# A tower of attention and experts on one core: the two attention terms moved through two column halves of TensorE instead of one summed term

## What is computed

```python
q, k, v = (split_heads(x @ W + b) for W, b in ((Wq, bq), (Wk, bk), (Wv, bv)))
scores = einsum("bhqd,bhkd->bhqk", q, k) / sqrt(64)
scores = scores * where(int(abs(scores) * 1618) % 9 in (0, 3, 6), 1 / PHI, 1.0)
a = softmax(scores)
a = a * (sin(C1 * a) * exp(-(a * a) / PHI) + cos(C2 * a))      # C1 = 118.6, C2 = 1.94
h = h + concat_heads(a @ v) @ Wo + bo
```

## Time and profile before

| | us |
|---|---|
| median of 3 runs | 6793.55 |
| fastest, slowest of them | 6787.77, 19916.96 |
| the profiled execution | 6774.6 |
| its span | 6772.9 |

### The profile page before, as it was taken

The page is one execution under the profiler, slowest core; times in us unless marked ns, Lnnn a source line. Parts: engine busy times, 40 slices in busy tenths (PEclk is TensorE's granted clock), DMA queues, the critical chain, the costliest instruction groups (busy, mean ns, idle before and its releaser), DMA issues. The chain is left out here.

```text
span 6772.9 us, 115321 instructions
## 1 busy us (share of the span) xinstructions
PE 5442.1 (80%) x32426; PEld 3955.2 (58%) x32489; DVE 5082.3 (75%) x10177; ACT 4262.2 (63%) x7370; POOL 2754.5 (41%) x2639
## 2 busy tenths in 40 slices
PE   2788877787777877877888777778787799997999
PEld 1455555555555555555655555555555577775777
DVE  1888888888888888888888888888888555555443
ACT  1677777777777777777777777777777322222222
POOL 4445554444555544444555444445554200100111
PEclk9888898989889888888888889888988799898999
DMA  1000000000000000000000000000000000000000
GB/s 17 12 8 7 7 7 7 7 7 10 7 7 7 7 7 7 7 9 9 7 7 7 7 7 7 9 9 7 7 7 4 8 1 2 1 1 13 4 6 6
DMA packets 34500, 48.46 MB, mean 7 GB/s; under 512 B 24473, under 2 KB 24537, under 8 KB 34010
## 3 DMA queue, kind: packets, MB, share of 16 engines
q1 hardware_dynamic: 31962, 43.49, 2.5%
q0 software_dynamic: 2048, 0.14, 0.1%
HBM read 39.40 MB, written 4.19 MB: 6 GB/s over the span
## 5 line engine op out<-in xcount | busy, mean ns | idle before, releaser
L571 PE MATMUL banks<-ident,att 128*128 128x128 f32 x8192 | 1458.9, 311 | 873.6 <-DVE ag L508 496.8
L571 PEld LDWEIGHTS banks<-ident,att 128*128 128x128 f32 x8192 | 1024.2, 159 | 1568.6 <-DVE ag L508 1044.0
L377 POOL TENSOR_TENSOR sinb<-sinb,work 128x512 f32<-128x512 f32 x1024 | 1289.3, 1272 | 900.3 <-DVE sinb L482 898.3
L599 PE MATMUL banks<-kT,qT 128*128 128x512 f32 x2048 | 1262.5, 702 | 113.9 <-ACT att L423 104.0
L387 POOL TENSOR_SCALAR wgt<-wgt 128x512 f32<-128x512 f32 x1024 | 700.2, 684 | 1586.7 <-DVE wgt L502 1581.4
L635 PEld LDWEIGHTS outp<-vo,sinb 128*128 128x128 f32 x8192 | 1164.7, 216 | 214.9 <-issue 185.3
L635 PE MATMUL outp<-vo,sinb 128*128 128x64 f32 x8192 | 1162.6, 295 | 1.9 <-ACT att L423 1.9
L476 DVE TENSOR_TENSOR work<-banks,work 128x512 f32<-128x512 f32 x1024 | 699.8, 689 | 254.0 <-ACT work L435 183.6
L451 ACT ACTIVATE work<-banks 128x512 f32<-128x512 f32 x1024 | 609.9, 596 | 420.4 <-PE banks L571 411.6
L458 ACT ACTIVATE mag<-banks 128x512 f32<-128x512 f32 x1024 | 606.4, 594 | 356.2 <-PE banks L599 350.0
L435 ACT ACTIVATE work<-banks,halfpi 128x512 f32<-128x512 f32 x1024 | 695.4, 685 | 208.9 <-PE banks L571 139.6
(11 more groups left out here) (194 smaller groups left out, 6740.6 us busy)
## 6 DMA issues: line engine op xcount, KB each, us to landing
xq<-xT_dram SPq DMA_DIRECT2D x64, 256.0 KB
xv<-xT_dram SPq DMA_DIRECT2D x64, 256.0 KB, 3.7
xT_dram<-xT SPq DMA_DIRECT2D x8, 256.0 KB, 2.9
out<-hres SPq DMA_DIRECT2D x8, 256.0 KB, 2.6
base<-in_L_tok_turns,idx POOLq DMA_INDIRECT x64
wqk<-in_L_attn_Wq SPq DMA_DIRECT2D x64, 16.0 KB
wqk<-in_L_attn_Wk SPq DMA_DIRECT2D x64, 16.0 KB
wqk<-in_L_attn_bq SPq DMA_DIRECT2D x64, 0.2 KB
```

Source lines behind the costliest of these rows:

```text
L377: nc.gpsimd.tensor_tensor(sinb[:, k % RING], sinb[:, k % RING], work[:, k % RING], ALU.add).then_inc(summed, 1)
L571: mm = nc.tensor.matmul(bank[:, i * P:(i + 1) * P], att[:, p, 4 * half + i, kt * P:(kt + 1) * P], ident[:], is_transpose=True, start=(i == ...
L599: nc.tensor.matmul(score_bank(n), qT[:, p, (n // 2) * P:(n // 2 + 1) * P], kT[:, p, (n % 2) * 512:(n % 2 + 1) * 512], start=True, stop=Tru ...
```

## The change

The two terms are no longer summed on GpSimd. Both go into TensorE as moving operands of 512 columns, with `vo` of the key block (128 x 64) as the stationary one: `work` writes partitions 0 to 63 of `outp`, `sinb` partitions 64 to 127. Each of the two matmuls so uses one half of the array's columns. The result is transposed, 64 x 512 queries for each term, so one query half fills the bank, and tiles are taken half by half: tile k is key block k % 8 and query half k // 8, for Gauss and sine too. VectorE takes each half out of `outp` (semaphore `evac`) into `acc`; an even head copies, an odd one adds to it. After the odd head eight matmuls with `pair`, two identities one above the other, fold both terms and turn the result back into 128 queries x 64 (`folded`), and VectorE adds that into `hres`, once for two heads. 

kT exists once: an even head has its q and k in rows 0 to 63, an odd one in rows 64 to 127, and the other half of its qT is zeros, so scores contract over 128 rows, of which the other head's k meets zeros. A head's projection is therefore put behind the last score of the head before (24 and 26 instead of 18 and 20), with the wait for all 16 scores, and the values move from 25 to 29. The rings `work` and `sinb` are freed by `av`, not by the sum. The diff, cut to its core:

```diff
-        kT = sb("kT", [P, 2, S])
+        kT = sb("kT", [P, S])
+        acc = sb("acc", [P, 2, 512])
+        pair = sb("pair", [P, D])
...
-        PROJ, VAL = 18, 25 + STEPS
+        PROJ, VAL = 24, 29 + STEPS
...
-        AV = [SINE + 6 + 8 * k // 5 for k in range(NTILE)]
-        OUT = AV[-1] + 1
+        AV = [SINE + 6 + k if k < TB else SINE + 16 + 2 * (k - TB) for k in range(NTILE)]
+        OUT = (AV[TB - 1] + 1, AV[-1] + 1)
+        FOLD, ADD = OUT[1] + 1, OUT[1] + 2
...
-                        k = a - SINE - 5
-                        if 0 <= k < NTILE:
-
-                            wait(pool, tmul, NTILE * g + k + 1)
-                            nc.gpsimd.tensor_tensor(sinb[:, k % RING], sinb[:, k % RING], work[:, k % RING],
-                                                    ALU.add).then_inc(summed, 1)
...
-                    wait(act, qk, NTILE * (g - 1))
+                    wait(act, qk, NTILE * g)
                 cols = slice(c * 512, (c + 1) * 512)
-                nc.scalar.activation(qT[0:D, p, cols], outp[0:D], ACT.Copy, scale=QSCALE).then_inc(qk_sb, 1)
-                nc.scalar.activation(kT[0:D, p, cols], outp[D:P], ACT.Copy).then_inc(qk_sb, 1)
+                rows = slice(p * D, (p + 1) * D)
+                nc.scalar.activation(qT[rows, p, cols], outp[0:D], ACT.Copy, scale=QSCALE).then_inc(qk_sb, 1)
+                nc.scalar.activation(kT[rows, cols], outp[D:P], ACT.Copy).then_inc(qk_sb, 1)
...
-                        if a == OUT:
-                            wait(dve, av, NTILE * (g + 1))
+                        if a in OUT:
+                            half = OUT.index(a)
+                            wait(dve, av, NTILE * g + TB * (half + 1))
+                            if p == 0:
+                                nc.vector.tensor_copy(acc[:, half], outp[:]).then_inc(evac, 1)
+                            else:
+                                nc.vector.tensor_tensor(acc[:, half], outp[:], acc[:, half], ALU.add).then_inc(evac, 1)
+                        if a == ADD and p == 1:
+                            wait(dve, folded, folds(g, p) + 1)
                             hv = hres[:, bass.ds((g // H) * TB, TB), :]
                             nc.vector.tensor_tensor(hv, outp[:].rearrange("p (t d) -> p t d", d=D), hv,
                                                     ALU.add).then_inc(outd, 1)
...
                             wait(pe, acd, NTILE * g + k + 1)
-                            wait(pe, turned, TB * (g + 1))
-                            kt, half = k // 2, k % 2
+                            wait(pe, turned, TB * g + 4 * (k // TB) + 4)
+                            kt, half = k % TB, k // TB
...
-                            fill(g, p, gauss_bank(d), d // 2, d % 2)
+                            fill(g, p, gauss_bank(d), d % TB, d // TB)
...
-                            wait(pe, summed, NTILE * g + k + 1)
+                            kt, half = k % TB, k // TB
+
+                            wait(pe, acd, NTILE * g + k + 1)
+                            wait(pe, tmul, NTILE * g + k + 1)
                             if k == 0:
                                 wait(pe, v_sb, g + 1)
-                            kt, half = k // 2, k % 2
-                            for i in range(4):
-                                o = (4 * half + i) * D
-                                mm = nc.tensor.matmul(outp[:, o:o + D], sinb[:, k % RING, i * P:(i + 1) * P],
-                                                      vo[:, kt, :], start=(k == 0 and i == 0),
-                                                      stop=(k >= NTILE - 2), skip_group_check=True)
+                            if k == TB:
+                                wait(pe, evac, 2 * g + 1)
+                            for term, rows in ((work, slice(0, D)), (sinb, slice(D, P))):
+                                mm = nc.tensor.matmul(outp[rows], vo[:, kt, :], term[:, k % RING],
+                                                      start=(kt == 0), stop=(kt == TB - 1), skip_group_check=True)
                             mm.then_inc(av, 1)
+                        if a == FOLD and p == 1:
+                            wait(pe, evac, 2 * g + 2)
+                            for j in range(TB):
+                                mm = nc.tensor.matmul(outp[:, j * D:(j + 1) * D],
+                                                      acc[:, j // 4, j % 4 * P:(j % 4 + 1) * P], pair[:],
+                                                      start=True, stop=True)
+                            mm.then_inc(folded, 1)
```

More of the change, by code:

```diff
@@ L316, in stages, with folds @@
                     yield g, (par - stage) % 2, s + STEPS * stage
+        def folds(g, p):
+            if isinstance(g, int):
+                return g // 2
+            return (g - p) // 2
         def score_bank(n):
@@ L365, in _ @@
             pool.wait_ge(consts, 5)
-            nc.gpsimd.memset(qT[D:P], 0.0).then_inc(consts, 1)
+            nc.gpsimd.tensor_tensor(pair[:], ident[:, 0:D], ident[:, D:P], ALU.add).then_inc(consts, 1)
             pool.wait_ge(consts, 6)
-            nc.gpsimd.memset(kT[D:P], 0.0).then_inc(consts, 1)
+            nc.gpsimd.memset(qT[:], 0.0).then_inc(consts, 1)
+            pool.wait_ge(consts, 7)
+            nc.gpsimd.memset(kT[:], 0.0).then_inc(consts, 1)
             def iteration(t, par):
@@ L393, in _ @@
         def _(act):
-            act.wait_ge(consts, 7)
+            act.wait_ge(consts, 8)
             def projections(g, p, c):
@@ L433, in iteration @@
                             else:
-                                wait(act, summed, NTILE * g + k - RING + 1)
+                                wait(act, av, NTILE * g + k - RING + 1)
                             nc.scalar.activation(work[:, k % RING], sine_bank(k), ACT.Sin,
@@ L447, in iteration @@
                             if d < RING:
-                                wait(act, summed, NTILE * g - RING + d + 1)
+                                wait(act, av, NTILE * g - RING + d + 1)
                             else:
@@ L549, in _, with project @@
         def _(pe):
-            pe.wait_ge(consts, 7)
-            def project(g, c):
+            pe.wait_ge(consts, 8)
+            def project(g, p, c):
                 wait(pe, loadq, 80 * (g + 1))
                 if c == 0:
-                    wait(pe, outd, g - 2)
+                    wait(pe, evac, 2 * (g - 2))
+                    wait(pe, outd, folds(g - 2, p))
                 else:
@@ L643, in iteration @@
                             wait(pe, qk_sb, 4 * NHEADS if last else 4 * (g + 3))
-                            wait(pe, outd, g)
+                            wait(pe, evac, 2 * g)
+                            wait(pe, outd, folds(g, p))
                             for j in range(TB):
```

16 lines of the change are left out of this document (8 added, 8 removed).

## The result

The changed kernel takes 7148.85 us in the median of 4 runs (7129.88 to 7185.85) against 6790.66: ratio 1.0537, interval 1.0482 to 1.0593, slower by 358 us (the ratio leaves out the one run of the kernel before at 19916.96 us). 7275 had been forecast, in a range of 6920 to 7620.

What follows compares the result with a forecast made beforehand. No engine was full: VectorE bound the score and Gauss stretch, a ring across engines the sine stretch. Terms 5.9 + 0.9 - 0.6 + 0.5 + 0.9 = +7.6 us a head, times 63 +480 us: about 7275 us, range 6920 to 7620.

Steps and rivals of the forecast that it cites:

- the side of 2%: Whole kernel: 2%, 136 us, is about what a measurement can tell from no change; slower than that had chance 0.83.
- TensorE becomes the bound of eight sine steps: Sine stretch, first eight attention-value tiles: a TensorE step grows from 1.55 to 2.29 us, +5.9 us a head.
- The pair of matmuls: Attention-value tile: two column-half matmuls take 1.28 us, with 0.30 for the change of form 1.58 us a tile.
- A2 and B1: A and B are a tile's two matmuls, 1 and 2 their passes; only second of A and first of B overlap.
- rival 2: Attention-value matmuls: the column halves run wholly together, +3.6 us a head, about 7020 us; chance 0.18.
- Projections and values: Turn from Gauss to sine: projection copies move behind the last score and values move later, +0.9 us a head.
- the table load (1.28 us) and the first cosines cover that: Start of sine: value matmuls at s = 29 hold transposes and L586 behind them, but this is hidden; no cost added.
- Late tiles and fold: Score and Gauss stretch: tiles at s = 12 and 14 and the fold at s = 16, together +0.9 us a head.
- Order by halves: Gauss stretch: TensorE no longer waits at the second tile, but VectorE is the full engine there; 0, upper bound 0.
- Contention: VectorE's L497 beside GpSimd's L382: without the sums the scalings start earlier and stop slowing it, -0.6 us a head.
- VectorE's additions: PSUM operations into acc and hres, 2.5 a head instead of 1, in score and sine stretches: +0.5 us a head.

Runs made afterwards that it cites:

- e12: The changed kernel with the first eight attention-value tiles two at a time in every second sine step; 7258.96 us, ratio 1.0698.
- e6: The kernel before with only its projection moved to steps 24 and 26 and its value matmuls to 29; 6975.44 us (one run).
- e13: The changed kernel with the Gauss tiles computed in the old order, key block d // 2 and query half d % 2; 7082.04 us, ratio 1.0426.
- e7: The changed kernel with a sum of the same size, read by nobody, put back on GpSimd; 7167.16 us, ratio 1.0568.
- e4: The changed kernel with one whole-array matmul a tile, leaving out the sine term and mixing key blocks; 7040.5 us (one run).
- e5: The changed kernel with values at step 21, fold in four pairs, first eight attention-value tiles spread over nine steps; 7022.38 us, ratio 1.0356.
- e1: The changed kernel with the value matmuls at step 20, ahead of the projection, instead of 29; 7030.07 us, ratio 1.036.
- e3: The changed kernel with both terms written to the same 64 partitions, through one column half, one after the other; 7651.39 us (one run).

## Why the prediction was right, and where not

The direction, the side of 2% and the range held, and so did the mechanism that TensorE becomes the bound of eight sine steps (12.52 of 12.52 us busy). How the passes fall within a step did not, and two terms were far off in opposite senses, so that a total within 2% of the measured one is partly luck.

- **The pair of matmuls.** "Passes start in program order, so ... only A2 and B1 lie next to each other" failed. A1 and B1 start together, and A2 and B2. The pair takes 0.86 us (e12), not 1.28, the change of form 0.25 (0.30 by the earlier trace rows). A step is 1.78 us instead of 2.29, so the sine stretch costs +2.0 us a head and not +5.9. That was rival 2, with 0.18. The Trainium skill's sentence that tiles are independent and work in parallel ("TensorEngine Tiling (Array Packing)", Key Properties) is what the trace shows, with 10 ns between their starts; and its rule that a changed mode drains TensorE agrees with 0.25 us for in and out.
- **Projections and values, +0.9 forecast.** e6 gives +3.4. The failed step is "the table load (1.28 us) and the first cosines cover that": the value matmuls had no price in the sum. Placed at the start of the sine stretch they took 3.3 us, in front of the third fill, and the cover was two cosines long. By the traces of e6 some 1.7 us of the 2.9 come from the place in the queue and 1.2 from the half clock, which they had in most heads there; the earlier trace rows gives 0.89 as the mean clock of the attention, and I used no clock of the place where the block would stand. The copies cost about 0.4 and not 0.9.
- **Late tiles and fold, +0.9.** The size came out (+1.03 from e6 to the changed kernel in the Gauss stretch), the reasons only half. With the clock of e13 late tiles and fold together leave the stretch where e6 has it (30.21 and 30.22 us). What they cost in the changed kernel is what TensorE loses at the half clock behind them: 0.71 us a head where a fold stands, 0.25 at the same step without one. No term of the sum was for that.
- **Order by halves, "0. Upper bound 0 as well".** Wrong here: e13 wins 1.0 us a head without it. The argument looked at who waits, and not at the clock at which TensorE would run behind the reordered tiles. Why order and clock go together is open, and e12 shows that they need not.
- **Contention, -0.6.** -0.27 by e7, 0.93 in the whole stretch; the rest is open. The mechanism, scalings that start earlier once the sums are gone, is what e7 shows.
- **VectorE's additions, +0.5.** Not separable; e4 leaves +0.26 in the sine stretch beyond the kernel before, in which their part there is contained.
- **Sum.** +7.6 forecast, +5.8 measured: 3.9 too much at the matmuls, 2.5 too little at the values; the other terms together make the remaining 0.4.

None of the versions beats the kernel before; the best, e5, is at 1.0356. e1 and e13 together were not run.

## What to carry to other kernels

A small block of matmuls is priced where it is put, not where it was: look first at what stands behind it in the queue and how much room the step has (1.7 us of e6's 2.9), then read the granted clock and the length of a neighbour there (1.2). In this kernel two products on the same engine, each in its own column half, ran at the same time, and this saved half their passes. Taking work off an engine that is on no ring (GpSimd here, 20 us a head) bought less than a microsecond a head, while each thing moved to make it possible had to find room in a step that has some.

## What the runs showed of the hardware

- Two float32 matmuls of 512 columns into column halves 0 to 63 and 64 to 127: each term's first pass starts 10 ns from the other's, each second pass too, and the pair takes 0.86 us (e12, 2023.13 to 2023.99). Into the same half a step is 0.85 us longer (e3).
- Going from the whole array to halves and back costs 0.25 us of TensorE (e4 and e12).
- The same eight 64-column float32 matmuls, sixteen passes, took 1.73 us at a granted clock of 1.00 (e13) and 3.30 at 0.50 (changed kernel). Both folds came behind a stretch in which TensorE was mostly waiting, busy 1.32 of 3.40 and 1.12 of 3.56 us, at 1.00: the busy share just ahead didn't tell which of the two clocks followed.
- VectorE's float32 tensor_scalar of 128 x 512 took 417 ns in the mean beside no GpSimd instruction and 795, up to 1195, beside GpSimd's scaling of 128 x 1024 float32 (changed kernel, 2000 to 4000 us).
